# A first attention's side work laid anew over its eight steps, its output projection in halves, and its maxima turned in another bank

## The chip, the cores and the metric

The kernel runs on 1 core of one Trainium2 chip. The metric is the device time of one execution in microseconds (us), as the median of several. Five engines run side by side: TensorE (PE, with its weight loads as PEld), VectorE (DVE), ScalarE (ACT), GpSimd (POOL) and SyncE (SP), which issues nearly all transfers. They meet in semaphores alone.

## The reference

Two layers, each a cross attention and a feed-forward block, on x (16 batches of 100 tokens, 256 wide) and a context (16 x 361 x 192). The change touches the first attention only:

```python
q = (layernorm(x) @ Wq + bq)   # 16 heads of 16
k = (ctx @ Wk + bk);  v = (ctx @ Wv + bv)
attn = clip(q @ k.T * 16**-0.5, -1e4, 1e4)
attn = softmax(attn)           # over the 361 keys of the same batch
attn = where(any(isnan(attn)), 1/361, attn)
x = x + (attn @ v) @ Wo + bo
```

Behind it come a mixture of eight experts with a shared one, a second attention with weights of three values, and a gated cell.

## The kernel before, in words

**The loop.** The first attention runs over the batches b. `over_batches` writes out the first two and the last four and puts the others into a hardware loop of two batches a turn (b = 2t + p; p and q = 1 - p name the halves of double buffers). A body (`a_tensor`, `a_scalar`, `a_vector`, `a_gpsimd`, one for each engine, and `a_sync`, which is written out for all 16) has eight steps i, one for two heads. `has(b, n)` is whether batch b + n exists, `from_(b, n)` whether b is at least n.

**The scores, twice.** The scores are needed with queries in rows, for the maximum over keys, and with keys in rows, for the product with v. Body b does for its own batch: `t_tensor` (t: scores with keys in rows, for two heads, into banks 4 and 5, three blocks of keys and one of `floor_k`), `exp_scalar` (exp: both banks into p32), `clip_vector` (clip), and on every second step `pv_tensor` (pv: a group of four heads, summed in bank 6). For batch b + 1 it does `s_tensor` (s: scores with queries in rows, two heads, banks 0 to 3) and `s_vector` (the reduction to maxima m32). There is one pair of banks for t, so t(i+1) waits for exp(i).

**The maxima.** A half of the maxima (eight heads) is clamped (`m_vector`), turned (`m_tensor`: a transpose on TensorE into bank 7), copied as fp16 (`m_scalar`), its low part formed (`m_low`) and written by SyncE (`rows_store`, qs<-mT, semaphore `mr_in`) into two rows of qs. t(0) waits for the rows of half 0, t(4) for those of half 1.

**The side work.** For batches ahead: k (`k_tensor`, chunks c0 and c1), v (`v_tensor`, two parts), q (`q_tensor`), and for batch b - 2 the output projection y (`y_tensor`, fp32, eight matmuls, then `y_vector` adds it to x). All of them, and the maxima's transpose, take turns in one bank, bank 7 (`UB_`): each is given the semaphore and count of the evacuation before it (`free`). `k_scalar`, `v_scalar`, `q_scalar`, `m_scalar` evacuate on ScalarE, where they stand in one order with the exponentials. `k_high` and `k_gpsimd` split k in two fp16 parts, `q_gpsimd` q, `c_scalar` and `c_gpsimd` the context.

**The transfers.** k and q go to memory (`k_store`, k_parts<-kp, one for each chunk; `q_store`) and come back into ks and qs (`half_load`: K and Q of half 0 or 1 of the heads, semaphores `kq_in` and `k1_in`). A `k_store` waits until the one before it has landed (`k_out`). The denominators go out and back: `den_load`, `inv_vector`, `inv_store`, and `inv_load` (rden<-inverse), which spreads a 4 x 400 table over 128 partitions; `on_gpsimd` waits for it and multiplies, and y waits for that. SyncE carries all of it out in the order of `a_sync`, waiting for each item's semaphores, and after bodies 9 to 12 also reloads a quarter of x each (0.4 MB).

Of the kernel before, what the change touches and what calls it, by code (L numbers as in the profile page):

```python
# [48 lines left out]
def build(nc, a, out):  # L49
    ctx = ExitStack()  # L50
    with ctx:
# [212 lines left out]
        UH_ = UB_[:, :].bitcast(F16)  # L264
# [18 lines left out]
        m_max, m_c, m_mm, m_h, m_l = (sem(f"m_{n}") for n in ("max", "c", "mm", "h", "l"))  # L283
# [12 lines left out]
        NP, HALF = H // 2, H // 4  # L296
# [223 lines left out]
        def t_tensor(pe, b, p, i):  # L520
# [116 lines left out]
        def a_tensor(pe, b, t, p):  # L637
            q = 1 - p
            for i in range(NP):
# [28 lines left out]
                if i == 7 and has(b, 2) and not has(b, 3):  # L668
                    guard_sums_tensor(pe, (y_x, b - 1))
                if i == 1 and has(b, 1) and not has(b, 2):  # L670
                    guard_even_tensor(pe, (m_l, 2 * b + 2))
                if i == 7 and has(b, 3):
                    k_tensor(pe, b + 3, q, 0, (y_x, b - 1) if from_(b, 2) else (q_32, b + 4))

        def a_scalar(s, b, t, p):
            q = 1 - p
            for i in range(NP):
                if i == 0 and has(b, 2):
                    k_scalar(s, b + 2, p, 0)
                if i == 1:  # L680
                    m_scalar(s, b, 1)
                if i == 2 and has(b, 2):
                    k_scalar(s, b + 2, p, 1)
                if i in (3, 4) and has(b, 1):
                    v_scalar(s, b + 1, q, i - 3)
                if i == 5 and has(b, 1):
                    m_scalar(s, b + 1, 0)
                if i == 6 and has(b, 3):
# [8 lines left out]
                if i in (0, 2) and has(b, 2):  # L697
                    k_high(s, b + 2, i // 2)
                if i in (4, 5) and has(b, 3):
                    c_scalar(s, b + 3, q, t + 1 + p, i - 4)  # L700

        def a_vector(v, b, t, p):
            q = 1 - p
            for i in range(NP):
# [4 lines left out]
                if i == 1:  # L709
# [2054 lines left out]
```

## Time and profile before

| | |
|---|---|
| median of 3 runs | 958.87 us (958.62 to 961.48) |
| the profiled execution | 962.21 us, its span 960.4 |
| TensorE / weight loads | 794.5 us (83%) / 583.8 (61%) |
| VectorE / ScalarE / GpSimd | 719.2 (75%) / 555.5 (58%) / 303.2 (32%) |
| chain that ended last | PE 49%, DVE 27%, ACT 9%, issue 7%, DMA 4% |
| exp (L536) | 128 of 834 ns, first at 55.0, last at 338.1 |
| first attention, with its opening | about 0 to 345 us |

A row of a timeline reads: start, duration, engine, line, operation, output<-input, shapes, and in brackets the idle time before it with what ended it. The line names are those of the kernel printed above. A row of the windows view gives for a stretch the busy time of each engine with its instructions, the granted TensorE clock, the mean share of the 16 DMA engines that was busy, and GB/s. The page marks matmul ends as modelled, so starts are compared rather than ends.

### The profile page before, as it was taken

Reading aid. Unit: us, or ns where it says so; the run is one execution under the profiler, and the core shown is the slowest. Engines: PE = TensorE matmul, PEld = TensorE weight load, DVE = VectorE, ACT = ScalarE, POOL = GpSimd, SP = SyncE. Lnnn points to the kernel's source line nnn. Section 1 sums busy time; section 2 is a strip of 40 time slices with the busy share of each in tenths; the row PEclk is TensorE's granted clock in tenths of the full one; section 3 lists DMA queues with packets and bytes.
Section 4 is the critical chain, followed back from the end, with each engine's and each line's share of the span. In section 5 each row is a group of like instructions: output and inputs, shape, how many; then the busy total and the mean of one; then the engine's idle time right before and its main releaser. Section 6 shows DMA issues by size and latency. Waiting matters only on the chain.

```text
span 960.4 us, 22060 instructions
## 1 busy us (share of the span) xinstructions
PE 794.5 (83%) x8198; PEld 583.8 (61%) x8198; DVE 719.2 (75%) x1456; ACT 555.5 (58%) x1150; POOL 303.2 (32%) x246
## 2 busy tenths in 40 slices
PE   3678888898898768879889999996555999869995
PEld 1355666666665545667657777783213777449994
DVE  7788777878887998767586666655696998767865
ACT  6356766666665436634366555636797776672532
POOL 6156453444551506031232220003641111243400
PEclk9799999999999776989999999997555999889998
DMA  6423443334443246404176654454210000200002
GB/s 169 102 66 82 107 101 98 104 93 114 119 114 85 80 143 224 160 25 133 37 208 185 179 168 146 123 135 140 65 47 10 1 2 1 89 1 2 3 2 69
DMA packets 76898, 89.53 MB, mean 93 GB/s; under 512 B 22150, under 2 KB 64929, under 8 KB 76826
## 3 DMA queue, kind: packets, MB, share of 16 engines
q1 hardware_dynamic: 69994, 80.50, 30.4%
q0 software_dynamic: 6144, 7.42, 3.0%
q8 instruction: 45, 0.74, 0.3%
q10 hardware_dynamic: 688, 0.66, 0.3%
q14 instruction: 27, 0.22, 0.1%
HBM read 72.87 MB, written 15.43 MB: 92 GB/s over the span
## 4 chain that ended last, share of the span: by engine, by line
PE 49%; DVE 27%; ACT 9%; issue 7%; DMA 4%; SPq 1%; POOL 1%; ACTq 0%; another core or an unknown queue 0%; DVEq 0%
PE ps L1183 11%; PE ps L1170 9%; PE ps L557 3%; PE ps L357 3%; PE ps L455 3%; PE ps L529 3%; DVE p L545 2%; PE ps L599 2%; DVE m L515 2%; PE ps L2195 2%; PE ps L510 2%; DMA k_parts<-kp 2%; DVE pmax L1652 2%; PE ps L2206 2%; DVE area L1778 1%
## 5 line engine op out<-in xcount | busy, mean ns | idle before, releaser
L515 DVE TENSOR_REDUCE m<-ps 100x2 f32<-100x722 f32 x128 | 115.6, 904 | 48.4 <-PE ps L510 46.5
L536 ACT ACTIVATE p<-ps 128x800 f32<-128x800 f32 x128 | 106.8, 834 | 42.6 <-PE ps L529 39.8
L1232 ACT ACTIVATE hT<-ps,cols 128x500 f32<-128x500 f32 (+1 forms) x96 | 62.5, 651 | 107.8 <-PE ps L1170 94.4
L1183 PE MATMUL ps<-w_h,hT_h 128*125 128x256 f16 (+1 forms) x384 | 105.5, 275 | 7.4 <-DVE x L1279 6.8
L1239 DVE TENSOR_TENSOR hT_l<-hT,hT_h 128x500 f16<-128x500 f32 (+1 forms) x96 | 62.3, 652 | 60.9 <-ACT hT_h L1233 59.2
L545 DVE SCALAR_TENSOR_TENSOR p<-p 128x600 f32<-128x600 f32 x128 | 107.2, 839 | 0.0
L1183 PE MATMUL ps<-w_h,hT_l 128*125 128x256 f16 (+1 forms) x384 | 105.4, 274 | 0.0
L1183 PE MATMUL ps<-w_l,hT_h 128*125 128x256 f16 (+1 forms) x384 | 105.4, 274 | 0.0
L1075 POOL DMA_INDIRECT xe<-tokens,slot_of x32 | 44.5, 1391 | 154.4 <-PE ps L1193 100.7
L1170 PE MATMUL ps<-xe_h,w_h 128*128 128x500 f16 (+1 forms) x192 | 72.5, 378 | 13.8 <-ACT hT_h L1233 5.6
L529 PE MATMUL ps<-qs,ks 128*128 128x100 f16 x768 | 63.0, 211 | 15.9 <-ACT p L536 15.1
L1170 PE MATMUL ps<-xe_l,w_h 128*128 128x500 f16 (+1 forms) x192 | 72.1, 376 | 0.0
L1170 PE MATMUL ps<-xe_h,w_l 128*128 128x500 f16 (+1 forms) x192 | 72.0, 375 | 0.0
L529 PEld LDWEIGHTS ps<-qs,ks 128*128 128x128 f16 x768 | 50.9, 99 | 30.0 <-ACT p L536 20.5
L510 PE MATMUL ps<-ks,qs 128*100 128x361 f16 x256 | 62.7, 329 | 7.0 <-DMA qs<-q_parts 5.4
L375 POOL TENSOR_TENSOR kp<-k,kp 128x361 f16<-128x361 f32 x32 | 31.4, 981 | 98.7 <-ACT kp L371 98.5
L1233 ACT ACTIVATE hT_h<-ps,cols 128x500 f16<-128x500 f32 (+1 forms) x96 | 62.0, 646 | 0.0
L1183 PEld LDWEIGHTS ps<-w_h,hT_h 128*125 128x125 f16 (+1 forms) x384 | 51.3, 134 | 12.3 <-DVE x L1279 6.0
L557 PE MATMUL ps<-p,v 128*32 128x100 f32 (+1 forms) x1536 | 48.9, 262 | 9.2 <-DVE p L545 9.0
L1183 PEld LDWEIGHTS ps<-w_l,hT_h 128*125 128x125 f16 (+1 forms) x384 | 51.4, 134 | 2.7
L1183 PEld LDWEIGHTS ps<-w_h,hT_l 128*125 128x125 f16 (+1 forms) x384 | 51.3, 134 | 0.0
L557 PEld LDWEIGHTS ps<-p,v 128*32 128x32 f32 (+1 forms) x1536 | 34.0, 114 | 27.4 <-DVE p L545 19.5
(344 smaller groups left out, 2128.0 us busy)
## 6 DMA issues: line engine op xcount, KB each, us to landing
sw<-in_L_ffn_w_dram SPq DMA_DIRECT2D x16, 512.0 KB
sw<-in_L_ffn_w_dram SPq DMA_DIRECT2D x8, 1024.0 KB, 5.8
k_parts<-kp SPq DMA_DIRECT2D x32, 192.0 KB, 2.7
ks<-k_parts SPq DMA_DIRECT2D x32, 192.0 KB
stage<-in_L_xattn_W_f_dram SPq DMA_DIRECT2D x6, 1024.0 KB
ctx_f<-in_ctxT_dram SPq DMA_DIRECT2D x16, 270.8 KB, 3.2
stage<-in_ctxT_dram SPq DMA_DIRECT2D x8, 541.5 KB
area<-in_ctxT_dram SPq DMA_DIRECT2D x16, 270.8 KB, 6.2
```

Of the source, the lines that this page charges most:

```text
L510: mm = pe.matmul(bank[at + n][0:T, 0:KV], qs[p][:, h, :], ks[p][:, h, 0:KV], start=True, stop=True)
L515: v.tensor_reduce(m32[p][:, 2 * i:2 * i + 2], ps[0:T, at:at + 2, 0:KV], AX.X, ALU.max).then_inc(m_max, 1)
L529: mm = pe.matmul(bank[t_bank(i) + n][:, j * T:(j + 1) * T], keys, qs[p][:, h, :], start=(j == 0), stop=True, skip_group_check=True)
L536: s.activation(p32[:, i % HALF, :, :, :].rearrange("p j n t -> p n j t"), ps[:, t_bank(i):t_bank(i) + 2, 0:(KJ + 1) * T].rearrange("p n (j ...
L545: v.scalar_tensor_tensor(probs, probs, 1.0, low, ALU.min, ALU.max).then_inc(a_cv, 1)
L557: i = pe.matmul(OB_[HR * r:HR * (r + 1), g * T:(g + 1) * T], v32[p][0:m, j, h, :], p32[0:m, h // 2 % HALF, j, h % 2, :], start=(g == 0 and ...
L1075: g.indirect_dma_start(xe[e % 2][:, j, :], None, x_d, bass.IndirectOffsetOnAxis(ap=slot_of[:, 4 * e + j:4 * e + j + 1], axis=0)).then_inc( ...
L1170: i = pe.matmul(bank[2 + f % 2][:, 0:width(n)], w1p[ww][:, k, f * 128:(f + 1) * 128], xep[p][xx][:, k, 0:width(n)], start=(k == 0 and ww = ...
L1183: i = pe.matmul(bank[4 + j % 3][0:m, 0:C], hTp[p][hh][:, f, j * m:(j + 1) * m], w2p[of][ww][:, f, :], start=(f == 0 and hh == ww), stop=(f ...
L1232: s.activation(hT[:, f % 3, 0:m], bank[2 + f % 2][:, 0:m], ACT.Silu, bias=bias, scale=1.0 / WS)
L1233: s.activation(hTp[p][0][:, f, 0:m], bank[2 + f % 2][:, 0:m], ACT.Silu, bias=bias, scale=1.0 / WS).then_inc(f_s, 1)
L1239: v.tensor_tensor(hTp[p][1][:, f, 0:m], hT[:, f % 3, 0:m], hTp[p][0][:, f, 0:m], ALU.subtract).then_inc(f_l, 1)
```

## The change

Five things.

1. The side work's places. k(c0) of batch b + 2 was issued in step 7 of the body before (for b + 3), now in step 0; k(c1) moves from step 1 to 2, v's first part from 2 to 1, its second stays in 3, q moves from 5 to 4; the last pv group but one moves behind y's second half in step 7. The evacuations on ScalarE, the splits on ScalarE (`k_high` of c1: step 2 to 5; the context: 4 and 5 to 6) and on GpSimd (`k_gpsimd` 1 and 3 to 2 and 6; q 7 to 5; the context 5 and 6 to 7) follow.
2. y in two halves of four matmuls, in steps 6 and 7; `y_vector` moves behind step 7's reduction.
3. The maxima. `m_vector` now makes both fp16 parts in [100 x 16], in three instructions. `m_tensor` is one fp16 matmul with a unit matrix, between t's two heads in steps 1 and 5, into unused columns of bank 4; `m_scalar` copies all 16 rows after the same step's exponential, and t(2) and t(6) wait for it. `m_low` goes.
4. SyncE's order: `inv_load` ahead of `rows_store` of half 1; `inv_store` and then `k_store` of c1 behind half 0's loads and rows.
5. Four bodies are written out ahead of the loop, where there were two. The opening makes a fp16 unit matrix and no longer k(c0) of batch 2.

```diff
+        m_hl = sba("m_hl", [T, 2 * NP], F16)
+        mT = sba("mT", [2 * NP, 2, T], F16)
+        ident_h = sba("ident_h", [T, T], F16)
+        M_OPEN, M_TURN = UB_[0:2 * NP, 0:T], bank[4][0:2 * NP, (KJ + 1) * T:(KJ + 2) * T]
...
         def m_vector(v, b, p, half):
+            top = m32[p][:, half * NP:(half + 1) * NP]
             v.wait_ge(m_max, NP * b + HALF * (half + 1))
             wait(v, m_mm, 2 * b + half)
-            v.scalar_tensor_tensor(m32c[:, :], m32[p][:, half * NP:(half + 1) * NP], CLAMP, least[:, :], ALU.min, ALU.max
-                                   ).then_inc(m_c, 1)
+            v.scalar_tensor_tensor(m32c[:, :], top, CLAMP, least[:, :], ALU.min, ALU.max).then_inc(m_c, 1)
+            v.scalar_tensor_tensor(m_hl[:, 0:NP], top, CLAMP, least[:, :], ALU.min, ALU.max).then_inc(m_c, 1)
+            v.wait_ge(m_c, 3 * (2 * b + half) + 2)
+            v.tensor_tensor(m_hl[:, NP:2 * NP], m32c[:, :], m_hl[:, 0:NP], ALU.subtract).then_inc(m_c, 1)
-        def m_tensor(pe, b, half, free):
-            turn_free(pe, free)
-            pe.wait_ge(m_c, 2 * b + half + 1)
-            pe.transpose(UB_[0:NP, 0:T], m32c[:, :], ident[0:T, 0:T]).then_inc(m_mm, 1)
+        def m_tensor(pe, b, half, at, start=False):
+            pe.wait_ge(m_c, 3 * (2 * b + half) + 3)
+            pe.matmul(at, m_hl[:, :], ident_h[:, :], start=start, stop=True, skip_group_check=True).then_inc(m_mm, 1)
...
         def rows_store(sp, b, p, half):
             wait(sp, mr_in, 32 * (2 * b + half))
+            sp.wait_ge(m_h, 2 * b + half + 1)
             for n in range(2):
-                sp.wait_ge((m_h, m_l)[n], 2 * b + half + 1)
-                sp.dma_start(qs[p][ROW_M + n:ROW_M + n + 1, half * NP:(half + 1) * NP, :], mT[:, half, n, :]
-                            ).then_inc(mr_in, 16)
+                sp.dma_start(qs[p][ROW_M + n:ROW_M + n + 1, half * NP:(half + 1) * NP, :],
+                             mT[n * NP:(n + 1) * NP, half, :]).then_inc(mr_in, 16)
...
         t_tensor:
             wait(pe, a_p, NP * b + i)
+            if i == 2:
+                pe.wait_ge(m_h, 2 * b + 2)
+            if i == HALF + 2 and has(b, 1):
+                pe.wait_ge(m_h, 2 * b + 3)
...
+                if n == 0 and i == 1:
+                    m_tensor(pe, b, 1, M_TURN)
+                if n == 0 and i == HALF + 1 and has(b, 1):
+                    m_tensor(pe, b + 1, 0, M_TURN)
...
         a_tensor:
-                if i % 2 and i >= 3:
-                    pv_tensor(pe, b, p, (i - 3) // 2)
+                if i == 0 and has(b, 2):
+                    k_tensor(pe, b + 2, p, 0, (y_x, b - 2) if from_(b, 3) else (q_32, b + 3))
                 if i == 1 and from_(b, 1):
                     pv_tensor(pe, b - 1, q, NQ - 1)
-                if i == 0:
-                    m_tensor(pe, b, 1, (k_32, 2 * b + 5) if has(b, 2) else (yb_ev, 3) if has(b, 1) else (y_x, b - 2))
                 if i == 1 and has(b, 2):
-                    k_tensor(pe, b + 2, p, 1, (m_l, 2 * b + 2))
-                if i in (2, 3) and has(b, 1):
-                    v_tensor(pe, b + 1, q, i - 2, (v_ev, 2 * b + 3) if i == 3 else
-                             (k_32, 2 * b + 6) if has(b, 2) else (yb_ev, 4))
-                if i == 4 and has(b, 1):
-                    m_tensor(pe, b + 1, 0, (v_ev, 2 * b + 4))
-                if i == 5 and has(b, 3):
-                    q_tensor(pe, b + 3, q, (m_l, 2 * b + 3))
+                    v_tensor(pe, b + 1, q, 0, (k_32, 2 * b + 5))
+                if i == 2 and has(b, 2):
+                    k_tensor(pe, b + 2, p, 1, (v_ev, 2 * b + 3))
+                if i in (3, 5):
+                    pv_tensor(pe, b, p, (i - 3) // 2)
+                if i == 3 and has(b, 1):
+                    v_tensor(pe, b + 1, q, 1, (k_32, 2 * b + 6) if has(b, 2) else (v_ev, 2 * b + 3))
+                if i == 4 and has(b, 3):
+                    q_tensor(pe, b + 3, q, (v_ev, 2 * b + 4))
                 if i == 6 and from_(b, 2):
-                    y_tensor(pe, b - 2, (q_32, b + 4) if has(b, 3) else
-                             (m_l, 2 * b + 3) if has(b, 1) else (m_l, 2 * b + 2))
+                    y_tensor(pe, b - 2, (q_32, b + 4) if has(b, 3) else (v_ev, 2 * b + 4) if has(b, 1) else (y_x, b - 2),
+                             range(0, HG // 2))
+                if i == 7 and from_(b, 2):
+                    y_tensor(pe, b - 2, None, range(HG // 2, HG))
+                if i == 7:
+                    pv_tensor(pe, b, p, 2)
-                if i == 7 and has(b, 3):
-                    k_tensor(pe, b + 3, q, 0, (y_x, b - 1) if from_(b, 2) else (q_32, b + 4))
...
         a_sync:
-            rows_store(sp, b, p, 1)
             if b >= 2 and has(b, 1):
                 inv_load(sp, b - 2)
+            rows_store(sp, b, p, 1)
...
             if has(b, 2):
-                k_store(sp, b + 2, t + 1, p, 1)
                 sp.wait_ge(a_s, NP * b + HALF)
                 half_load(sp, b + 2, p, 0)
             if has(b, 1):
                 rows_store(sp, b + 1, q, 0)
+            if b >= 1:
+                inv_store(sp, b - 1)
+            if has(b, 2):
+                k_store(sp, b + 2, t + 1, p, 1)
             if has(b, 4):
                 context_load(sp, b + 4, p)
-            if b >= 1:
-                inv_store(sp, b - 1)
```

## Rows read from the trace of the kernel before

**Rows 1.** Busy time by engine in one body, clock, DMA share, GB/s.
```profile
157.79:175.36 17.57, 15.68 (x228) 11.07 (x228) 13.76 (x23) 11.66 (x30) 7.61 (x8) 1.00 0.39 100
```
**Rows 2.** Timeline of ScalarE: first exponentials of b = 1, 2, 13, 14.
```profile
72.81 0.83 ACT L536 ACTIVATE p<-ps 128x800 f32<-128x800 f32 x1
...
92.46 0.83 ACT L536 ACTIVATE p<-ps 128x800 f32<-128x800 f32 x1
...
286.50 0.83 ACT L536 ACTIVATE p<-ps 128x800 f32<-128x800 f32 x1
...
302.81 0.84 ACT L536 ACTIVATE p<-ps 128x800 f32<-128x800 f32 x1 [1.64 <-PE ps L529]
```
**Rows 3.** Timeline of ScalarE: the first two exponentials of b = 5.
```profile
145.46 0.83 ACT L536 ACTIVATE p<-ps 128x800 f32<-128x800 f32 x1
...
146.91 0.84 ACT L536 ACTIVATE p<-ps 128x800 f32<-128x800 f32 x1
```
**Rows 4.** The chain of waits in the same body: start, duration, what.
```profile
145.37 0.19 ACT k L365
...
147.18 0.65 PE ps L557 x24
147.84 1.04 PE ps L357 x6
...
149.69 1.48 PE ps L455 x12
151.17 0.36 PE ps L529 x8
151.53 0.31 PE ps L510 x2
...
152.49 0.79 PE ps L455 x6
...
156.37 0.65 PE ps L391 x12
...
157.95 1.97 PE ps L599 x8
```
**Rows 5.** Groups of instructions from 122.67 to 227.97: busy, mean ns, idle before.
```profile
L515 DVE TENSOR_REDUCE m<-ps 100x2 f32<-100x722 f32 x48 | 43.5, 906 | 18.2 <-PE ps L510 17.3
...
L545 DVE SCALAR_TENSOR_TENSOR p<-p 128x600 f32<-128x600 f32 x48 | 37.0, 772 | 0.0
...
L630 POOL TENSOR_TENSOR ctxl<-ctx_f,ctxh 96x361 f16<-96x361 f32 x13 | 18.0, 1389 | 5.2 <-ACT ctxh L625 5.2
...
L408 POOL TENSOR_TENSOR qp<-q,const 128x200 f16<-128x200 f32 x6 | 9.8, 1630 | 0.5
...
L478 DVE SCALAR_TENSOR_TENSOR m32c<-m,least 100x8 f32<-100x8 f32 x12 | 3.6, 300 | 0.0
L411 POOL TENSOR_TENSOR qp<-q,qp 128x200 f16<-128x200 f32 x6 | 3.4, 563 | 0.5
```
**Rows 6.** Timeline of SyncE's queue in b = 6.
```profile
165.85 0.56 SPq L587 DMA_DIRECT2D rden<-inverse  x1
166.52 0.42 SPq L382 DMA_DIRECT2D k_parts<-kp  x1
...
171.29 0.38 SPq L382 DMA_DIRECT2D k_parts<-kp  x1
```
**Rows 7.** Timeline of GpSimd in b = 6.
```profile
171.02 1.03 POOL L593 TENSOR_TENSOR on<-o,rden 128x400 f32<-128x400 f32 x1 [1.36 <-DMA rden<-inverse]
```
**Rows 8.** Busy time by engine in stretches of 1 us, as rows 1.
```profile
168.30:169.30 1.00, 1.00 (x15) 0.73 (x12) 0.42 (x1) 0.93 (x4) 0.51 (x1) 1.00 0.19 59
169.30:170.30 1.00, 1.00 (x28) 0.81 (x28) 0.85 (x2) 0.81 (x2) 0.36 (x1) 1.00 0.26 95
```
**Rows 9.** The tile k_parts over the whole span: its stores from issue to landing.
```profile
DMA to landing us min/median/max: 2.0/2.7/7.5
```
**Rows 10.** The chain of waits in b = 12.
```profile
271.99 5.69 DMA rden<-inverse
```

More of the change, by code:

```diff
@@ L282, in build @@
         s_mm, a_s, a_p, a_cv, a_pv = (sem(f"a_{n}") for n in ("s1", "s", "p", "clip", "pv"))
-        m_max, m_c, m_mm, m_h, m_l = (sem(f"m_{n}") for n in ("max", "c", "mm", "h", "l"))
+        m_max, m_c, m_mm, m_h = (sem(f"m_{n}") for n in ("max", "c", "mm", "h"))
         mr_in = sem("m_rows_in")
@@ L649, in a_tensor @@
                     guard_flag_tensor(pe)
-                if i % 2 and i >= 3:
-                    pv_tensor(pe, b, p, (i - 3) // 2)
+                if i == 0 and has(b, 2):
+                    k_tensor(pe, b + 2, p, 0, (y_x, b - 2) if from_(b, 3) else (q_32, b + 3))
+                if i == 0 and has(b, 1) and not has(b, 2):
+                    guard_sums_tensor(pe, (y_x, b - 2))
                 if i == 1 and from_(b, 1):
                     pv_tensor(pe, b - 1, q, NQ - 1)
-                if i == 0:
-                    m_tensor(pe, b, 1, (k_32, 2 * b + 5) if has(b, 2) else (yb_ev, 3) if has(b, 1) else (y_x, b - 2))
@@ new lines, in a_tensor @@
+                if i == 1 and has(b, 1) and not has(b, 2):
+                    guard_even_tensor(pe, (yb_ev, 3))
+                if i == 2 and has(b, 2):
+                    k_tensor(pe, b + 2, p, 1, (v_ev, 2 * b + 3))
+                if i == 2 and has(b, 1) and not has(b, 2):
+                    v_tensor(pe, b + 1, q, 0, (yb_ev, 4))
+                if i in (3, 5):
+                    pv_tensor(pe, b, p, (i - 3) // 2)
+                if i == 3 and has(b, 1):
+                    v_tensor(pe, b + 1, q, 1, (k_32, 2 * b + 6) if has(b, 2) else (v_ev, 2 * b + 3))
@@ L677, in a_scalar @@
             for i in range(NP):
[L678 to L688, printed above, removed]
+                if i in (1, 3) and has(b, 2):
+                    k_scalar(s, b + 2, p, i // 2)
+                if i == 1 and has(b, 1) and not has(b, 2):
+                    guard_sums_scalar(s)
+                if i == (2 if has(b, 2) else 3) and has(b, 1):
+                    v_scalar(s, b + 1, q, 0)
+                if i == 4 and has(b, 1):
+                    v_scalar(s, b + 1, q, 1)
+                if i == 5 and has(b, 3):
                     q_scalar(s, b + 3, q)
                 exp_scalar(s, b, i)
-                if i == 0 and has(b, 1) and not has(b, 2):
-                    guard_sums_scalar(s)
+                if i == 1:
+                    m_scalar(s, b, 1, M_TURN)
+                if i == 5 and has(b, 1):
+                    m_scalar(s, b + 1, 0, M_TURN)
+                if i in (1, 5) and has(b, 2):
+                    k_high(s, b + 2, i // 4)
                 if i == 2 and not has(b, 1):
@@ L696, in a_scalar @@
                     o_scalar(s, b - 1, q)
[L697 to L700, printed above, removed]
+                if i == 6 and has(b, 3):
+                    for c in range(2):
+                        c_scalar(s, b + 3, q, t + 1 + p, c)
         def a_vector(v, b, t, p):
@@ L708, in a_vector @@
                     m_vector(v, b + 1, q, 0)
-                if i == 1:
-                    m_low(v, b, 1)
-                if i == 5 and has(b, 1):
-                    m_low(v, b + 1, 0)
-                if i == 7 and from_(b, 2):
-                    y_vector(v, b - 2)
                 if has(b, 1):
@@ L720, in a_vector @@
                     guard_row_vector(v)
+                if i == 7 and from_(b, 2):
+                    y_vector(v, b - 2)
                 if i >= 1:
@@ L732, in a_gpsimd @@
             for i in range(NP):
-                if i == 1 and has(b, 2):
-                    k_gpsimd(g, b + 2, 0)
                 if i == 1 and not has(b, 1):
                     guard_even_gpsimd(g, 1)
+                if i == 2 and has(b, 2):
+                    k_gpsimd(g, b + 2, 0)
                 if i == 3:
-                    if has(b, 2):
-                        k_gpsimd(g, b + 2, 1)
                     on_gpsimd(g, b - 2, p) if from_(b, 2) else x_bias_gpsimd(g, 2 * b)
@@ L743, in a_gpsimd @@
                             guard_even_gpsimd(g, n)
+                if i == 4 and not from_(b, 2):
+                    x_bias_gpsimd(g, 2 * b + 1)
+                if i == 5 and has(b, 3):
+                    q_gpsimd(g, b + 3)
+                if i == 6 and has(b, 2):
+                    k_gpsimd(g, b + 2, 1)
+                if i == 7 and has(b, 3):
+                    for c in range(2):
+                        c_gpsimd(g, b + 3, q, c)
                 if i == 7 and has(b, 1) and not has(b, 2):
                     guard_even_gpsimd(g, 0)
-                if i == 4 and not from_(b, 2):
-                    x_bias_gpsimd(g, 2 * b + 1)
-                if i in (5, 6) and has(b, 3):
-                    c_gpsimd(g, b + 3, q, i - 5)
-                if i == 7 and has(b, 3):
-                    q_gpsimd(g, b + 3)
         def a_sync(sp, b, t, p):
@@ L956, in over_batches @@
         def over_batches(eng, body):
-            for b in range(2):
-                body(b, 0, b)
-            with eng.Fori(1, B // 2 - 2) as t:
+            for b in range(4):
+                body(b, b // 2, b % 2)
+            with eng.Fori(2, B // 2 - 2) as t:
                 for p in range(2):
@@ L2382, in _ @@
             open_norm(v, 2)
+            v.wait_ge(const_in, 112)
+            vs.inc(v.tensor_copy(ident_h[:, :], ident[0:T, 0:T]))
+            vs.sync(v)
             for i in range(NP):
```

34 lines of the change are left out of this document (12 added, 22 removed).

## The prediction

> **What bounds the kernel now.** I read the busy shares (table above), then one body of the attention loop engine by engine. TensorE is busy for 15.68 of the 17.57 us of a body (one batch), at full clock, VectorE for 13.76 [rows 1]. The starts of each body's first exponential give the pace: 11 bodies from 92.46 to 286.50, mean 17.64; the unrolled ends differ, 19.65 for b = 1, 16.31 for b = 13 [rows 2].
>
> Inside a body each step i goes over one pair of banks: t(i) on TensorE, exp(i) on ScalarE, then t(i+1). Exponentials follow each other at 1.45 us when nothing else is in the way (145.46 to 146.91) [rows 3]; eight such steps would be 11.6. The other 6 us are TensorE's extras and waits. The chain of waits prices the extras: t 0.36, s 0.31, pv 0.65, k 1.04, v 1.48 and 0.79, q 0.65, y 1.97 [rows 4]. With 8 t, 8 s, 4 pv, 2 k, both v, q and y that is 14.9. The rest is standing still: in steps 0 and 4, which have no extra but a small transpose (about 0.7 each), and where an extra's evacuation sits ahead of an exponential on ScalarE, so that the chain goes through ACT k L365 [rows 4]. VectorE's reduction (0.91) and clip (0.77) [rows 5] make its load.
>
> **The change part by part.** I write one steady body again from T0, the start of t(0), with these durations. exp(i) starts at least 0.56 after t(i), and t(i+1) 0.88 after exp(i), its 0.83 and the semaphore (rows 3: 1.45 = 0.56 + 0.88).
>
> Step 0 gets k(c0). Its context parts come late: c_scalar moves behind exp(6), and its two POOL subtractions (1.39 each) behind q_gpsimd (1.63 and 0.56) and k_gpsimd (an estimate of 1, its shape being near c's) [rows 5], so they end about 1.2 after T0: k starts there and, 0.93 without its drain, t(1) goes at 2.1. Next late is VectorE: y_vector now waits for y's second half in step 7, then clip(6), the longer m_vector and the reduction stand one behind another, and clip(7) ends near 2.8; pv(3) starts at 2.9, just where TensorE would be too (2.1 + 0.36 + 0.05 + 0.31 + 0.1). Both delays fall on one place and cost 0.5 once.
> pv and v (1.32 without drain): t(2) at 4.9. k(c1) waits for v's activation: t(3) at 6.65. pv and v's rest: t(4) at 8.8. q in step 4 is hidden by exp(4): t(5) at 10.3. pv(1) waits 0.2 for clip(3), t(6) for the maxima's copy out of bank 4: 12.0. y in halves, 1.8 without drain, 0.9 each, plus 0.1 for each entry: t(7) at 13.6; and 13.6 + 0.67 + 1.0 + 0.65 = **15.9** is the next T0. From t(4) to there it is 7.1.
>
> Maxima: the transpose and its waits in bank 7 go; a small fp16 matmul stands between t's matmuls. I take 0.05 (one of t's eight: 0.36 / 8), bounded by nothing and by 0.25, one of y's eight fp32 matmuls. On VectorE m_vector grows from one small instruction (mean 0.30 [rows 5]) to three with a wait between, and the low part's goes. I take 0.5 for the three, with nothing more than now (0.30) and 0.9 (three means) as ends; VectorE has 2 us a body free, so only its place at T0 counts.
>
> SyncE's queue: inv_load(b-2) moves ahead of rows_store(b, half 1), and k_store(c1) behind inv_store, so that half 1's loads come later too. Now rden<-inverse is issued at 165.85 [rows 6] and on_gpsimd, which waits for it, runs at 171.02 [rows 7]: 5.1. While it drains the DMA share is 0.19 to 0.26 for 2.7 us [rows 8], so it holds 4 of 16 engines. k_parts<-kp, issued at 166.52 just behind, has not landed before 171.29, when the next store that waits for it goes out [rows 6]: 4.8, against 2.0 at the least and 2.7 in the middle for all such stores [rows 9]. So a transfer that shares those four engines ends 0.3 behind rden. The rows of the maxima (eight pieces) will now be issued behind rden. k_store(c1) goes at T0 - 0.9 and lands at 1.1 (the 2.0), the loads are issued from 1.15 to 2.8, rden at 2.85; it lands at 7.9 to 8.6 (5.1, or the 5.69 of a crowded body [rows 10]), the rows 0.3 later at 8.2 to 8.9. t(4) waits for them and wants to go at 8.8: they are just about on time. I add 0.2 a body: **16.1**.
> The Trainium skill, page "DMA: Bandwidth & Descriptors", section "Why a DMA increments its semaphore by 16 and not by 1", says that such a transfer runs on the largest number of engines up to 16 that divides the slowest dimension of both sides, always the lowest-numbered ones: 4 for rden, 8 for the rows, among them the same four. The trace agrees for rden by its share of 0.26; for the rows no row here shows it. By the rule the rows end behind rden in each body; on other engines they would have landed near 7.
>
> The x reloads (0.4 MB) that SyncE issues after bodies 9 to 12 will stand between k_store(c1) and the loads, with all of it ahead of rden. Around one of them rden took 5.69 though issued later [rows 10]. I take 1.5 more for b = 10 to 12, 17.6 (ends 15.9 and 20), and 17.0 for b = 13, which has less besides.
>
> The other moved issues have room: half 0's loads go out at about T0 + 9 for an s(0) at 16.4, where now they go behind the store of 171.29 for one at 180.0; half 0's rows have 3.9 us from their copy to t(0), against that middle of 2.7. q_store comes earlier. Two more bodies unrolled cost nothing, since unrolled and looped ones now share one pace [rows 2].
>
> **Sum.** b = 2 to 12: 194.0 becomes 8 x 16.1 + 3 x 17.6 = 181.6: -12.4. b = 13: +0.7. b = 0 and 1 (y missing, but POOL's bias additions still stall VectorE): -2.7 together, an estimate from the steady 1.5 each. Opening: k(2, c0) no longer precedes the first exponential: -1.0, its own 1.04. b = 14, 15 and the tail, which lose some waits for bank 7: -1.0. Together **-16.4**. Everything behind waits for the last y_x, its weight loads too, and moves with it. The profiled execution took 962.2 (span 960.4) and the median is 958.9, so 942.5; I say **943**.
>
> **Rivals.**
> (a) The rows are never late, also around the x reloads. For: while rden drains, the other twelve engines stand idle [rows 8]. Then 11 x 15.9 for 194.0, -19, b = 13 -0.4: 935.
> (b) The other side: rden's transfer becomes the bound. Place: t(4)'s wait for the rows, with all of TensorE behind it. From t(4) to the next T0 it is 7.1, so a body is slower than 17.57 once the rows land later than T0 + 10.4. That needs rden's four engines to begin on it only when the loads' last piece is in (2.8 + 5.0 = 7.8, as long as rden itself takes) and to need their 2.7 then: rows at 10.8, body 18.0, with an x reload 20.6: +3.5, +9, +2 and the other terms' -4.7 make +10: 969. Against it: rden never took over 5.7 from its issue. Halfway (rows at 10.2, body 17.3, with x 19) it is 957 to 962.
> The rule of the Trainium skill's page "DMA: Bandwidth & Descriptors" named above is the one that speaks for (b).
> (c) The spread does nothing, since bank 7 is still one bank and k, v, k, v, q wait for each other's evacuation: body 17.3, 957. For it: k(c1) waits for v's copy. Against: each wait comes a step after its cause.
> (d) VectorE's longer m_vector and later y_vector cost 1.2 and not 0.5 near T0: body 16.6, 947.
>
> **How the numbers follow.** Forecast, 938 to 951 with (d) in it: 0.52. (a): 0.20. (b) in full 0.09, halfway 0.10. (c) 0.09. About 0.3% (3 us) is what a measurement of this kernel tells from no change. Faster, under 956: the forecast, (a), and some of (c): 0.78. Within 0.3%: halfway (b) and most of (c), 0.12. Slower: 0.10. The range leaves out no more than 2 in 10: from 932, all of (a), to 960, part of halfway (b).
>
> **What would show it.** Right: 16.1 between first exponentials, TensorE busy for over 0.95 of it; k's wait on ctxl and pv(3)'s on the clip, 0.2 to 0.6, ahead of t(2); t(4) waiting some tenths for qs<-mT and for no other transfer; on_gpsimd at T0 + 8 to 8.6. A t(4) that waits over 1 us for qs<-mT in each body makes (b) right; an exp(1) more than 3 us behind exp(0) makes (c) or (d) right; bodies 10 to 13 over 19 make my x term wrong. A later stage that gives time back would make the sum wrong though its terms hold.

## The result, and the profile after

The changed kernel takes 970.53 us in the median (967.95 to 975.45, 4 runs), the kernel before on the same chip 959.1 (958.62 to 961.48): a ratio of 1.013, 95% interval 1.011 to 1.015. It is slower by some 11 us, where I had forecast 16 us less. A second series of the changed kernel on another chip gave 1.011 (1.008 to 1.014). The profiled execution took 970.61 us, its span 968.7.

First the page: the span, the busy times, and the start of the chain that ended last.

```profile
span 968.7 us, 21974 instructions
...
PE 802.8 (83%) x8198; PEld 589.7 (61%) x8198; DVE 729.7 (75%) x1489; ACT 555.7 (57%) x1150; POOL 303.9 (31%) x246
...
PE 39%; DVE 23%; DMA 11%; ACT 8%; issue 8%; POOL 8%; SPq 2%; ACTq 0%; DVEq 0%; POOLq 0%
```

Work has hardly grown. The chain has changed its make-up: PE fell from 49% to 39%, DMA rose from 4% to 11%, POOL from 1% to 8%. So the time goes into waits for a transfer and for GpSimd. The body of b = 6, which answers to [rows 1], in the view of busy time by stretch:

```profile
163.76:181.76 18.00, 15.77 (x228) 11.18 (x229) 14.59 (x25) 11.66 (x27) 8.35 (x8) 1.00 0.39 97
```

TensorE's 15.77 us are those of before (15.68), in a body of 18.0 instead of 17.57. VectorE has 0.83 more, GpSimd 0.74. Next, ScalarE's timeline in that body: exp(0), exp(3) and exp(4) [rows 3].

```profile
164.40 0.84 ACT L544 ACTIVATE p<-ps 128x800 f32<-128x800 f32 x1 [1.39 <-PE ps L533]
...
171.94 0.83 ACT L544 ACTIVATE p<-ps 128x800 f32<-128x800 f32 x1
...
175.15 0.84 ACT L544 ACTIVATE p<-ps 128x800 f32<-128x800 f32 x1 [1.29 <-PE ps L533]
```

From exp(3) to exp(4) it is 3.21 us, in a step whose side work needs about 2. The chain of waits in the same stretch says why [rows 4]:

```profile
163.02 2.25 POOL ctxl L639 x2
...
165.39 1.11 PE ps L359 x6
...
167.95 0.22 ACT mT L494
...
168.26 0.65 SPq L501
...
168.96 5.42 DMA qs<-mT
...
174.51 0.53 PE ps L533 x8
```

The chain leaves TensorE twice: at T0 (163.76), where k(c0) waits for GpSimd's second context part until 165.39, and at t(4), which waits for half 1's rows until 174.51. SyncE's queue shows what stands ahead of those rows [rows 6], GpSimd's timeline when rden was in [rows 7]:

```profile
163.09 1.07 SPq L384 DMA_DIRECT2D k_parts<-kp  x1
...
165.83 0.41 SPq L435 DMA_DIRECT2D ks<-k_parts  x1
...
167.21 0.28 SPq L445 DMA_DIRECT2D qs<-q_parts  x1
167.58 0.58 SPq L595 DMA_DIRECT2D rden<-inverse  x1
168.26 1.33 SPq L501 DMA_DIRECT2D qs<-mT  x2
```

```profile
161.07 1.99 POOL L377 TENSOR_TENSOR kp<-k,kp 128x361 f16<-128x361 f32 x1
163.02 2.24 POOL L639 TENSOR_TENSOR ctxl<-ctx_f,ctxh 96x361 f16<-96x361 f32 x2
...
174.18 1.03 POOL L601 TENSOR_TENSOR on<-o,rden 128x400 f32<-128x400 f32 x1 [4.41 <-DMA rden<-inverse]
```

Loads, rden and rows are issued in one go, and rden is in just ahead of 174.18, 6.5 us after its issue; the rows are in at 174.38, right behind it. How the 16 DMA engines empty, in stretches of 1 us [rows 8]:

```profile
168.00:169.00 1.00, 1.00 (x14) 0.90 (x11) 1.00 (x2) 0.56 (x3) 0.36 (x1) 1.00 0.79 108
...
172.00:173.00 1.00, 1.00 (x28) 0.85 (x28) 1.00 (x2) 0.77 (x2) 0.00 (x0) 1.00 0.26 90
173.00:174.00 1.00, 0.43 (x4) 0.18 (x2) 0.88 (x4) 0.38 (x1) 0.00 (x0) 1.00 0.17 53
```

The share (the last but one column) is 0.26 and then 0.17: four engines, and fewer, work on while TensorE's busy time falls to 0.43. Last, the bodies with an x reload. First exponential of b = 10 with its exp(3) and exp(4), then the first of b = 13 and 14 (ScalarE's timeline, [rows 2]):

```profile
234.92 0.84 ACT L544 ACTIVATE p<-ps 128x800 f32<-128x800 f32 x1 [1.32 <-PE ps L533]
...
242.53 0.83 ACT L544 ACTIVATE p<-ps 128x800 f32<-128x800 f32 x1
246.67 0.84 ACT L544 ACTIVATE p<-ps 128x800 f32<-128x800 f32 x1 [2.22 <-PE ps L533]
...
293.00 0.84 ACT L544 ACTIVATE p<-ps 128x800 f32<-128x800 f32 x1 [1.29 <-PE ps L533]
...
313.96 0.84 ACT L544 ACTIVATE p<-ps 128x800 f32<-128x800 f32 x1 [1.45 <-PE ps L533]
```

Here exp(4) is 4.14 behind exp(3), and body 13 takes 20.96. TensorE's clock falls in such a body. Two stretches of b = 13, during t(4)'s wait (it goes at 303.75) and behind it:

```profile
303.00:304.00 1.00, 0.25 (x6) 0.26 (x7) 0.00 (x0) 0.00 (x0) 0.59 (x1) 1.00 0.10 22
...
308.00:309.00 1.00, 1.00 (x14) 0.87 (x11) 0.59 (x1) 0.07 (x1) 1.00 (x1) 0.50 0.11 37
```

The granted clock (the last column but two) is 1.00 up to 304, while TensorE is busy for 0.05 of the microsecond from 302 and 0.25 of the one from 303, and then 0.50 from 305 to 311, the lower of its two levels (1.2 GHz in place of 2.4). Over the whole body it is 0.84, in b = 10 and 11, where t(4) waits 2.0, it is 0.91. In the kernel before it is 1.00 in every body from b = 2 on.

From such rows of both kernels, start to start of the first exponentials:

| | before | after | difference | forecast |
|---|---|---|---|---|
| first exponential of b = 0 | 54.95 | 56.20 | +1.2 | -1.0 |
| b = 0, 1 | 37.5 | 36.9 | -0.6 | -2.7 |
| b = 2 to 9 | 141.4 | 141.8 | +0.4 | -12.6 |
| b = 10 to 12 | 52.6 | 58.1 | +5.5 | +0.2 |
| b = 13 | 16.3 | 21.0 | +4.7 | +0.7 |
| b = 14 to the end | | | -2.9 | -1.0 |
| span | 960.4 | 968.7 | +8.3 | -16.4 |

Of the 24.7 us between forecast and measured span, 13.0 stand in b = 2 to 9, 5.3 in b = 10 to 12 and 4.0 in b = 13. The first line and the last differ by 1 to 3 us between executions of kernels that share this code, so their differences can't be told from scatter: on one chip the first exponential came at 55.88 in e2, which has the opening of the kernel before, and at 54.2 to 54.4 in e1, e3 and e4.

### The profile page after: what moved, and what is told of

It reads as the page before. It is cut to its first block, busy times and chain, and to the rows that moved or that the text cites. A ratio compares the mean times of both kernels' runs of the same rounds, so it can differ in the third digit from the quotient of the medians.

```text
span 968.7 us, 21974 instructions
## 1 busy us (share of the span) xinstructions
PE 802.8 (83%) x8198; PEld 589.7 (61%) x8198; DVE 729.7 (75%) x1489; ACT 555.7 (57%) x1150; POOL 303.9 (31%) x246
## 4 chain that ended last, share of the span: by engine, by line
PE 39%; DVE 23%; DMA 11%; ACT 8%; issue 8%; POOL 8%; SPq 2%; ACTq 0%; DVEq 0%; POOLq 0%
PE ps L1194 11%; PE ps L1181 9%; DMA qs<-mT 7%; POOL ctxl L639 3%; PE ps L533 2%; PE ps L2206 2%; PE ps L359 2%; DVE p L553 2%; POOL kp L377 2%; PE ps L2217 1%; DVE area L1789 1%; PE ps L510 1%; DVE pmax L1663 1%; ACT area L2016 1%; POOL qp L413 1%
## 5 line engine op out<-in xcount | busy, mean ns | idle before, releaser
L553 DVE SCALAR_TENSOR_TENSOR p<-p 128x600 f32<-128x600 f32 x128 | 110.5, 866 | 0.0
L533 PE MATMUL ps<-qs,ks 128*128 128x100 f16 x768 | 69.1, 216 | 24.1 <-DMA qs<-mT 13.6
L533 PEld LDWEIGHTS ps<-qs,ks 128*128 128x128 f16 x768 | 49.5, 101 | 47.0 <-ACT p L544 16.3
L510 PE MATMUL ps<-ks,qs 128*100 128x361 f16 x256 | 64.9, 338 | 7.5 <-DMA qs<-q_parts 5.9
L377 POOL TENSOR_TENSOR kp<-k,kp 128x361 f16<-128x361 f32 x32 | 47.2, 1475 | 57.6 <-ACT kp L373 57.5
L533 PE MATMUL ps<-qs,floor_k 128*128 128x100 f16 x256 | 52.6, 215 | 0.0
```

The source lines that it names most:

```text
L377: g.tensor_tensor(kp[:, 1, c, 0:KV], k32[c][:, :], kp[:, 0, c, 0:KV], ALU.subtract).then_inc(k_l, 1)
L510: mm = pe.matmul(bank[at + n][0:T, 0:KV], qs[p][:, h, :], ks[p][:, h, 0:KV], start=True, stop=True)
L553: v.scalar_tensor_tensor(probs, probs, 1.0, low, ALU.min, ALU.max).then_inc(a_cv, 1)
```

## The experiments

The ratios are to the kernel before on the same chip, with 95% intervals. It took 966.4 us on the chip of e1 to e4, 958.8 on that of e5 to e8, 959.7 on that of e9 and e10 and 964.7 on that of e11, so ratios are compared and not times; a range of times in an expectation is meant for a kernel before of 959. "Gap 3 to 4" is the time from exp(3) to exp(4) in the middle bodies.

My theory after the result: t(4) waits for the rows because they share rden's four engines (rival (b) of the prediction). The rival to it: the loop through GpSimd (rden, `on_gpsimd`, q, k, context, k(c0)) sets the pace, and t(4)'s wait only hides that.

**e1: the rows ahead of rden**, in the changed kernel.

```diff
+            rows_store(sp, b, p, 1)
             if b >= 2 and has(b, 1):
                 inv_load(sp, b - 2)
-            rows_store(sp, b, p, 1)
```

> The changed kernel, with one edit: SyncE issues the maxima's rows of half 1 ahead of rden<-inverse again. Theory A (the rows end behind rden on rden's four DMA engines, and t(4) waits for them): t(4) goes 9.5 us after t(0) and not 10.75, the bodies of b = 2 to 9 take 16.75 and not 17.7, those of b = 10 to 13 about 17.3 and not 19.8; 952 to 956 us. Theory B (the rows are late because all of SyncE's queue is late, whatever stands directly ahead of them): the wait of t(4) shrinks by at most 0.6, bodies 17.3 or more; 964 to 971 us.

Measured: 967.25, ratio 1.000 (0.998 to 1.002). t(4)'s wait is gone (gap 3 to 4 is 1.98), but gap 0 to 1 has grown to 3.4, and bodies 4 to 12 take 17.5 in the mean (16.4 to 18.7). Bodies 10 to 13 take 70.6 in place of 79.0. The chain of waits of this kernel, from 197.3 on:

```profile
202.56 0.64 SPq L501
...
203.30 5.06 DMA rden<-inverse
...
208.52 1.04 POOL on L601
...
210.23 1.30 POOL qp L410
...
213.31 0.87 POOL kp L377
214.19 1.47 POOL ctxl L639
```

The rows no longer wait, but rden, issued 1.3 later, now ends last: through `on_gpsimd`, q, k and the context, one behind the other on GpSimd, it holds k(c0) of the next body, and that holds the next rows. Both theories are true, one behind the other: either order of SyncE leaves the other wait. The time that was expected for the first (0.993 to 0.997 as a ratio) did not come, because of the second wait.

**e2: the kernel before, with rden ahead of the rows**, the same two lines exchanged there.

> The kernel before, with one edit: rden<-inverse ahead of the maxima's rows of half 1, as in the changed kernel. Theory A with room: half 1's loads go out 0.8 us before t(0) here, rden right behind them at T0 + 1.0, so it lands near 6.2 and the rows near 6.7, and t(4) goes at 8.6: no wait, 957 to 961 us. The rival (this order costs by itself, wherever the loads are): t(4) waits about 1.2 us in each of 12 bodies, 970 us or more.

Measured: 969.71, ratio 1.003 (1.000 to 1.005), bodies of 17.87, no wait at t(4) but in b = 2 and b = 12. The order alone costs the kernel before at most half a per cent: there the rows have slack, with half 1's loads issued 1.1 ahead of t(0) in b = 6 of e2 and 2.1 behind it in the changed kernel. It is the order together with the later loads that hurts.

**e3: rden in four transfers of 32 partitions each**, in the changed kernel; the same bytes. (`inv_store` also waits for the rden before.)

```diff
-            sp.dma_start(rden[:, :],
-                         inv_d[:, None, :].broadcast_to((QUAD, HR, HG * T))).then_inc(rden_in, 16)
+            for r in range(QUAD):
+                sp.dma_start(rden[HR * r:HR * (r + 1), :],
+                             inv_d[r:r + 1, :].broadcast_to((HR, HG * T))).then_inc(rden_in, 16)
```

> The changed kernel, with rden<-inverse in four transfers of 32 partitions each, in place of one of 128 that reads a table of 4 rows; the order of the queue stays. Theory A (four engines hold it for 2.5 us each): over all 16 engines it holds each for 0.7 at most, and the rows come 1.2 to 1.8 us earlier though their issue is 1.2 later; bodies of b = 2 to 9 at 17.0, 955 to 960 us. Theory B (bytes ahead of them, not engines): no change, 968 to 973 us.

Measured: 964.89, ratio 0.998 (0.995 to 1.000); bodies 3 to 8 take 17.0, gap 3 to 4 is 1.98, in bodies 10 to 12 still 3.6 to 4.0 (10 to 13 take 73.9). SyncE's and GpSimd's timelines in b = 6, and the stretch in which most of rden drains:

```profile
162.81 1.70 SPq L597 DMA_DIRECT2D rden<-inverse  x4
...
168.13 1.99 POOL L603 TENSOR_TENSOR on<-o,rden 128x400 f32<-128x400 f32 x1 [2.69 <-DMA rden<-inverse]
```

```profile
165.00:166.00 1.00, 0.98 (x14) 0.58 (x12) 0.17 (x1) 0.83 (x2) 0.44 (x1) 1.00 0.71 184
```

From its first issue rden takes at most 5.3 instead of 6.5, though the last of its four parts goes out 1.3 later; and the rows behind it are in time. The width of rden is a cause, shown. The share of a stretch mixes all transfers, and it falls to 0.23 here too, in the microsecond from 166 with rden's last part. The packets tell them apart: rden's rows, and q's behind which they stand, are 1600 bytes each. In the changed kernel 3.7 such packets are under way at a time in the mean from 170.5 to 172.5, at 67 ns each; in e3 13 from 165.5 to 166.0, at 89 ns each. The Trainium skill, page "DMA: Bandwidth & Descriptors", section "Why a DMA increments its semaphore by 16 and not by 1", has the number of engines set by the slowest dimension of both sides, as the largest number up to 16 that divides both; by that rule it is 4 for one [4, 32, 400] transfer and 16 for one of 32 partitions. The trace agrees with the 4 by the share of 0.26 and the 3.7 packets at a time, and with more than 4 for the split by the 13.

**e4: the context's and k's splits earlier** on ScalarE (context behind exp(4) and exp(5), k(c1) behind exp(3)) and GpSimd (k, `on`, k, context, q, context), `k_store` of c1 ahead of `inv_store`; rden as in the changed kernel.

```diff
-                if i in (1, 5) and has(b, 2):
-                    k_high(s, b + 2, i // 4)
+                if i in (1, 3) and has(b, 2):
+                    k_high(s, b + 2, i // 2)
...
-                if i == 6 and has(b, 3):
-                    for c in range(2):
-                        c_scalar(s, b + 3, q, t + 1 + p, c)
+                if i in (4, 5) and has(b, 3):
+                    c_scalar(s, b + 3, q, t + 1 + p, i - 4)
```

> The changed kernel, with the context's splits back behind exp(4) and exp(5), k's second split behind exp(3), GpSimd in the order k, context, q, context, and k_store(c1) ahead of inv_store; rden still ahead of the rows. Theory A with a second wait: k(c0) no longer waits for ctxl (0.97 us from t(0)), k_store(c1) and the loads go out about 1 us earlier against t(0), so rden and the rows do too: bodies of b = 2 to 9 at 16.7, 955 to 960 us. If only TensorE's path shortens and not SyncE's, the wait of t(4) takes it all: 968 to 972 us.

Measured: 968.22, ratio 1.002 (0.998 to 1.006). Gap 0 to 1 is 1.85, so k(c0)'s wait is gone; bodies 4 to 9 take 17.0 in the mean; gap 3 to 4 is 2.5 to 3.6 and in bodies 10 to 13 4.4 to 4.9 (78.4 in all). The chain's `165.47 5.68 DMA qs<-mT` shows that t(4) still waits. The ratio lies between the two expectations (0.996 to 1.001, 1.009 to 1.014): the wait of t(4) takes part of the gain in the middle and nearly all of it in bodies 10 to 13 (78.4 for 79.0).

**e5: e4 with e1's order.**

> The changed kernel with both edits: the splits early (as e4_splits_early) and the rows ahead of rden (as e1_rows_first). Each alone left one wait of about 1.2 us in each body: e1 the one of k(c0) for ctxl, which came through rden, on_gpsimd and q_gpsimd, e4 the one of t(4) for the rows. Theory C (two waits that stand in for each other): only together they go, bodies of b = 3 to 9 at 16.0, b = 10 to 13 at 16.5, a ratio of 0.982 to 0.988 to the kernel before. The rival (GpSimd's line on, k, context, q, context is too long by itself with rden landing at T0 + 10.3): k(c0) still waits over 0.5, ratio 0.99 to 1.00.

Measured: 956.54, ratio 0.997 (0.995 to 0.999). Gap 3 to 4 is 1.98, gap 0 to 1 3.1, bodies about 17.2: as in e1, rden comes 1.3 later and then GpSimd's line, for all the earlier splits, ends behind T0. What it gains on e4 is the x reloads' part (68.6 instead of 78.4 for bodies 10 to 13). The expectation for both edits together (bodies at 16.0) is missed, and its rival came true.

**e6: e4 with e3's four transfers.**

> The changed kernel with the splits early and rden in four transfers over all engines, still ahead of the rows. Theory C: bodies of b = 3 to 9 at 16.0 too, but around the x reloads (b = 10 to 13) t(4) still waits for the rows, some 18.3 as in e3_rden_wide; ratio 0.987 to 0.993. The rival (step 0 of e3 is slow for another reason than ctxl): bodies at 17.0, ratio 0.997.

Measured: 954.12, ratio 0.996 (0.993 to 0.998). Neither wait is left in the middle, bodies 4 to 8 take 16.6 to 16.7, bodies 10 to 13 69.3. But gap 5 to 6 is 2.28, where e4 has 1.71: a third wait appears, which the expected 16.0 had not reckoned with. In bodies 10 to 12 t(4) still waits (gap 3 to 4 3.4 to 3.7).

**e7: the x reloads later**, in the middle of the next body, behind `den_load`; otherwise the changed kernel.

> The changed kernel, with each reload of x issued by SyncE in the middle of the next body (behind den_load, ahead of half 0's loads) in place of the end of its own. If the loss of b = 10 to 13 (19.8 on the mean, against 17.7 before them) is the reload's 0.4 MB ahead of loads, rden and rows, those four bodies take about 17.9: 7 us less than the changed kernel, ratio 1.004 to 1.008. If it is the tail's own doing (the written-out bodies), 1.011 to 1.014 as the changed kernel.

Measured: 960.69, ratio 1.003 (1.001 to 1.006). Bodies 10 to 13 take 69.3 in place of 79.0, 3 to 9 take 17.4 to 18.2, as in the changed kernel (17.4 to 18.0). The x reload ahead of rden and rows cost 9.7 us, most of the whole loss. That it is the place, not the bytes, is shown: they are the same. Part of the 9.7 is TensorE's clock: with the long waits gone it is 1.00 in all four bodies (see below).

**e8: e6 with e1's order**: early splits, wide rden, rows first.

> The changed kernel with all three: splits early, rows ahead of rden, rden over all engines. Bodies at 16.0 everywhere, b = 10 to 13 too: ratio 0.980 to 0.986. If rden's landing no longer matters once the splits are early, the same as e5_early_rows_first within 0.3%.

Measured: 951.33, ratio 0.993 (0.990 to 0.997), faster than both kernels and the lowest of all, though the intervals of e6 and e11 overlap with it. The expected 0.980 to 0.986 are missed. Bodies 5 to 9 take 16.6 to 16.8, b = 3 and 10 16.0 to 16.1, and 10 to 13 together 66.5. Most of the 0.7 between 16.0 and 16.7 stand at gap 5 to 6 (2.28 against 1.71). VectorE's timeline there, and GpSimd's:

```profile
170.29 0.77 DVE L553 SCALAR_TENSOR_TENSOR p<-p 128x600 f32<-128x600 f32 x1
170.99 1.00 DVE L481 SCALAR_TENSOR_TENSOR m32c<-m,least 100x8 f32<-100x8 f32 x1
171.91 0.15 DVE L482 SCALAR_TENSOR_TENSOR m_hl<-m,least 100x8 f16<-100x8 f32 x1
172.09 0.72 DVE L484 TENSOR_TENSOR m_hl<-m32c,m_hl 100x8 f16<-100x8 f32 x1
```

```profile
170.82 1.14 POOL L603 TENSOR_TENSOR on<-o,rden 128x400 f32<-128x400 f32 x1 [3.53 <-DMA rden<-inverse]
171.92 0.88 POOL L377 TENSOR_TENSOR kp<-k,kp 128x361 f16<-128x361 f32 x1
```

The 100 x 8 instructions take 1.00 and 0.72 us, where their medians are 0.16 and 0.17, and each ends when the GpSimd instruction beside it does: 171.99 by 171.96, 172.81 by 172.80.

**e10: e8, with GpSimd's step 3 behind the maxima**, to test that.

```diff
+                if i == 3 and has(b, 1):
+                    g.wait_ge(m_c, 3 * (2 * b + 2) + 3)
```

> e8_early_wide_rows_first with one wait more: GpSimd's on (or bias addition) in step 3 waits until m_vector has made the fp16 maxima of half 0. Theory D (m_vector's small instructions stand behind a GpSimd instruction that runs at the same time: 1.00 and 0.72 us in place of 0.16 and 0.17, and pv(1) then waits for clip(3)): they take 0.5 together again, step 5 to 6 takes 1.71 and not 2.28, bodies at 16.0 and not 16.7, ratio 0.985 to 0.990. If the small instructions are slow by themselves there: no change, 0.990 to 0.997.

Measured: 956.06, ratio 0.995 (0.993 to 0.998). VectorE's timeline:

```profile
176.46 0.16 DVE L481 SCALAR_TENSOR_TENSOR m32c<-m,least 100x8 f32<-100x8 f32 x1
176.54 0.16 DVE L482 SCALAR_TENSOR_TENSOR m_hl<-m,least 100x8 f16<-100x8 f32 x1
176.73 0.17 DVE L484 TENSOR_TENSOR m_hl<-m32c,m_hl 100x8 f16<-100x8 f32 x1
```

At its place the theory holds: 0.16, 0.16 and 0.17, and gap 5 to 6 is 1.71. But GpSimd's line then ends later, k(c0)'s wait is back in many bodies (gap 0 to 1 2.5 to 3.2), bodies 3 to 12 take 16.3 to 17.4, and nothing is gained (0.985 to 0.990 were expected). The Trainium skill, page "SBUF — State Buffer", section "Who interferes with whom", states that a VectorE instruction with two inputs in SBUF and a GpSimd instruction that reads SBUF exclude each other, and that the second waits for the first to end; the trace agrees with it by the two pairs of ends above. All of VectorE's clips and these three small ones are of that kind.

**e9: e8 with y whole in step 6 again.**

```diff
-                             range(0, HG // 2))
-                if i == 7 and from_(b, 2):
-                    y_tensor(pe, b - 2, None, range(HG // 2, HG))
+                             range(HG))
```

> e8_early_wide_rows_first with y in one piece in step 6 again (y_vector stays behind step 7's reduction). With halves steps 6 and 7 take 1.46 and 2.38 together with the next body's first; whole, step 6 takes 2.5 and step 7 about 1.5. Theory (the halves save only the idle time of an exponential-bound step 7): 0.1 to 0.3 us a body, within 0.4% of e8, ratio 0.992 to 0.998. If the halves were worth a whole exponential-bound step (0.7 a body) the ratio would be 1.002 or more.

Measured: 959.89, ratio 0.999 (0.996 to 1.002); bodies 17.4. Steps 6 and 7 together take what they took in halves (gap 6 to 7 is 2.31 for 1.46, 7 to 0 1.6 for 2.4), but gap 1 to 2 grows from 2.8 to 3.4. So the halves are worth 0.6 to 0.7 a body, more than the 0.1 to 0.3 expected, and in a step that I had not named; why there, the runs don't tell. (`y_vector` stays behind step 7's reduction here.)

**e11: e8 with the maxima's small matmul issued twice**; the first copy goes to columns of bank 5 that nobody reads.

```diff
+            if not start:
+                pe.matmul(bank[5][0:2 * NP, (KJ + 1) * T:(KJ + 2) * T], m_hl[:, :], ident_h[:, :], start=False, stop=True,
+                          skip_group_check=True)
```

> This is the kernel of e8 with the small fp16 matmul that turns the maxima issued twice in steps 1 and 5 of every body: the first copy goes to columns of bank 5 that nobody reads, the second is the one used. Nothing else changes. Theory 1 (the matmul lengthens t by about 0.25 us each, the 0.61 against 0.36 between t(1) and s(1) in the changed kernel, and not by the 0.05 of my sum, and these two steps are on TensorE's line): a second copy costs again 0.1 to 0.25 in each of the two steps, +0.2 to +0.5 us a body, 3 to 7 us in all: a ratio of 0.996 to 1.001 to the kernel before, with bodies of about 17.0. Theory 2 (the 0.25 is a wait for its operand or for the evacuation, and the matmul itself is nearly free): the second copy costs nothing, ratio as for e8 (0.990 to 0.9965) and bodies of 16.65.

Measured: 957.99, before on this chip 964.73, ratio 0.994 (0.992 to 0.995); bodies as in e8. TensorE's timeline in b = 6, t(1) to s(1):

```profile
161.64 0.30 PE L536 MATMUL ps<-qs,ks 128*128 128x100 f16 x3
161.78 0.21 PE L536 MATMUL ps<-qs,floor_k 128*128 128x100 f16 x1
161.91 0.21 PE L489 MATMUL ps<-ident_h,m_hl 100*16 100x100 f16 x1
161.96 0.21 PE L491 MATMUL ps<-ident_h,m_hl 100*16 100x100 f16 x1
162.10 0.31 PE L536 MATMUL ps<-qs,ks 128*128 128x100 f16 x3
...
162.29 0.47 PE L513 MATMUL ps<-ks,qs 128*100 128x361 f16 x2
```

My theory on record for it fell. The second copy starts 0.05 after the first; the distances on either side, 0.13 and 0.14, are there once for both. From t to s it is 0.65, 0.61 with one copy, 0.36 with none. So the matmul itself is worth the 0.05 of my sum, and the other 0.2 belong to going into it and out of it. Why those cost what they do the runs don't tell.

**The changed kernel again**, on the chip of e9 and e10.

> The changed kernel as it is, on the same chip as the two others of this call, so that they can be compared with it directly. Ratio to the kernel before 1.010 to 1.015, as first measured; bodies of b = 10 to 13 near 19.8.

Measured: 970.92, ratio 1.011 (1.008 to 1.014), bodies 10 to 13 at 78.8: the result stands.

## Why the prediction was wrong

**The step that failed** is the sizing in SyncE's queue: "k_store(c1) goes at T0 - 0.9 and lands at 1.1", and rden, issued at 2.85, "lands at 7.9 to 8.6". Measured in b = 6:

| after T0 | forecast | measured |
|---|---|---|
| k_store(c1) issued | -0.9 | -0.67 |
| first load issued | 1.15 | 2.07 |
| rden issued | 2.85 | 3.82 |
| rden in | 7.9 to 8.6 | at the latest 10.4 |
| rows in | 8.2 to 8.9 | 10.6 |
| t(4) could go | 8.8 | 9.7 |
| t(4) goes | 9.0 | 10.75 |
| next T0 | 16.1 | 18.0 |

Of the rows' 2 us one comes from the start: k_store(c1) is issued 0.2 later and it took 2.7 from there to the first load's issue, not the 2.0 that I had taken from the least of its kind [rows 9], whose middle was 2.7. I took the best case of a row that had its middle beside it. The other 0.8 to 1.4 are rden's own time: 6.5 from issue, where I allowed 5.1 to 5.7 [rows 7, 10]. Before, it is issued 2.8 after the last load is out; now 0.1 after it, behind all loads of a half. That was the condition that I had written beside rival (b), and held against it that rden "never took over 5.7 from its issue". It had never been issued there. The rival's mechanism is what happened, and I had given it 0.09 in full and 0.10 halfway. Its sizes hold in part. The body shown has them (rows at 10.6, t(4) waits 1.07, body 18.0), but its sign, a wait of over 1 us in each body, comes among the middle bodies in b = 3, 5 and 6 only (1.1); in b = 2, 4 and 7 to 9 t(4) waits 0.7 at the most, and the mean of b = 2 to 9 is 17.7, between halfway and full. That its total of 969 lies so near is partly luck: its terms are +3.5, +9, +2 and -4.7 (8 bodies of 18.0 against 141.4 make +2.6, not the +3.5), where the trace has +0.4, +5.5, +4.7 and -2.3. That rows share rden's engines, landing 0.3 behind (measured at least 0.2), and that from t(4) to the next T0 it is 7.1 (7.25) were right.

**The x reloads.** +1.5 a body was forecast on 16.1, measured is +1.6 for 10 to 12 on 17.7, but +3.3 in b = 13, where 17.0 in all was forecast. As the base moved, the term lands on a body that already waits. Of the 79.0 us for 10 to 13, e7 takes away 9.7: had they been issued behind `den_load`, the change would have been near no change.

One term of these bodies stands nowhere in the prediction, which takes TensorE at full clock throughout. Behind t(4)'s waits of 2.0 (b = 10, 11) and 1.7 (b = 13) the granted clock goes down to 0.50 for some microseconds; behind that of 2.3 in b = 12 it stays at 1.00. From t(4) to the next T0 it is then 8.2, 8.1 and 9.6, against 7.3 in b = 4 to 9 and 7.1 in b = 12 and in e3's b = 13, all at 1.00. So some 4.3 of the 79.0 us are the slower clock and not the wait itself. The second profile of the changed kernel has the same in b = 11, 12 and 13 (8.1, 8.1, 8.4, clock 0.91 in each body). No run holds the clock fixed, so the 4.3 is an estimate from these distances.

**GpSimd's line.** I had k(c0) at T0 + 1.2 and a small wait for the context. It went at T0 + 1.6 and, once the rows' wait was taken away, at T0 + 2.4 (e1: t(0) at 196.67, k(c0) at 199.03). I never followed the line rden, `on_gpsimd`, q, k, context as one: it holds the body at about 17.2 to 17.5 by itself (e5, e1). In part its instructions got longer: kp took 0.89 in the middle over the span before and 1.23 after (the tile's median), 1.99 in the body shown; the context's parts got shorter (1.36 before, 0.88 after), so that GpSimd's busy time is the same over the span (303.2, 303.9).

**The maxima.** On VectorE m_vector took 1.15 in step 0 of that body (0.83, 0.15, 0.17), above my upper end of 0.9, beside GpSimd's context parts. It cost nothing there: it ended at 165.56, and the small matmul that reads it went at 166.60, behind k(c0). The small matmul costs 0.25 a place, as my upper bound.

**What was right.** In part the spread itself. With the rows in time and everything else as predicted (e3) a body takes 17.0, not the 15.9 that I had worked out with no late rows: exp(1) comes 2.7 to 2.9 behind exp(0), by the context's wait. Only with the splits moved earlier as well (e6, e8), which is not the change that I priced, a body takes 16.65, and 16.0 where VectorE and GpSimd don't meet. That 16.0 is so near 15.9 is no proof of my steps. Rival (c), that the spread does nothing, falls by these runs, and rival (d)'s size is the one that e8 shows, 0.7 a body, though in step 5 and not at T0. With e8 bodies 2 to 12 take 183.1 of the 194.0 before.

**What stays open.** Bodies 0 and 1 take 35.9 to 37.8 us in the kernels with the late splits, both kernels of the change among them, and 39.6 to 41.6 in those with the early ones. In these k(c1)'s split stands behind x's bias additions on GpSimd, 6.4 us in e8's trace; that this is the cause wasn't tried, nor a version that keeps the late order there, which might save e8 another 2 to 4 us. The granted clock is lower in the second of them too: 0.82 to 0.91 in b = 1 of every kernel with early splits, 1.00 in the changed kernel, e1, e3 and e7; which of the two is the cause, or both, is open. What is behind the last batch's first exponential takes 634 to 645 us over these kernels (638.9 before, 636.5 after). That goes with the chip and not with the edit: 642 to 645 in e1 to e4, 642 in e11, 634 to 637 in e5 to e10; what differs between the chips isn't known.

## What to carry to other kernels

A transfer that fills few DMA engines takes the time of its place in the queue, not its own: price it, and whatever small transfer stands behind it, as issued after all the bytes that the new order puts ahead, and take the middle of its landing times, not the least. When a wait is removed, follow the loop that comes next all round (here rden, GpSimd's six instructions, k, the rows) before writing down the gain: here three limits stood within 1.5 us of each other. Large loads that nobody needs soon go behind the small transfer that somebody waits for. And look at the granted clock of each body before a wait's length is taken for its cost.

## What the hardware showed that I had not expected

- A VectorE instruction of 100 x 8 elements took 1.00 us in place of 0.16 while GpSimd worked, and ended with GpSimd's instruction; after moving GpSimd's behind it, 0.16 again (e8, e10).
- The same 128 x 400 fp32 transfer took 5.1 us from issue before, 6.5 behind a half's loads, and at most 5.3 there when it was cut in four (e3).
- Behind three of four waits of TensorE of some 2 us the granted clock went from 1.00 to 0.50 for several microseconds, which cost another 0.9 in b = 10 and in b = 11 and 2.5 in b = 13 (an estimate from the distances above); the kernel before has 1.00 in every body from b = 2 to 14.
- A fp16 matmul with 16 columns of weights between t's matmuls costs 0.25, a second one directly behind it 0.05 (e11).
